# A state-space scan driven in place in its PSUM bank, in every iteration of a fused Mamba, attention and expert kernel

## The chip, the cores and the metric

The kernel runs on 1 core of one Trainium2 chip. The metric is the device time of one execution in microseconds (us). Before the change it is 1405.29 us, the median of 3 runs (1405.14 to 1409.21).

## The reference, cut to what matters

Eight images of 64 channels and 32x32 pixels go through three blocks: a selective state-space layer (Mamba) with group norm and residual, causal attention inside windows, and a mixture of eight experts of which each token takes two. The change lies in the first block, whose core is a recurrence over the 1024 tokens of an image, for 128 channels times 16 states:

```
def _selective_scan(xc, dt, Bmat, Cmat, A, D):
    def step(h, inp):
        dt_t, B_t, C_t, x_t = inp
        dA = jnp.exp(dt_t[..., None] * A)                        # "decay"
        dBx = dt_t[..., None] * B_t[:, None, :] * x_t[..., None] # "drive"
        h = dA * h + dBx                                         # "state"
        y = jnp.einsum('bdn,bn->bd', h, C_t)                     # "read", then "fold"
        return (h, y)
    ...
t = t + _L1_attn_ref(_ln_t(t), L1_attn_w_attn, L1_attn_w_proj)
t = t + _L1_ffn_ref(_ln_t(t), ...)
```

The 128 x 16 = 2048 recurrences of an image are 16 chunks of 128 rows, each row 1024 tokens long.

## The kernel before, in words

**A pipeline over images.** `pipeline` calls each engine's `program(a, c, p, b, f)` 12 times. In one iteration five images are in five stages: `c` is the image whose scan runs, `p` the one whose scan is being read out and normalised, `b` the one in attention, `f` the one in the experts. Eight images give iterations in which only some stages exist: in iterations 1 and 2 there is a scan without attention (`c` without `b`), in 3 scan and attention without experts, in 4 to 8 all of them, and from 9 on no scan.

**Two stages per iteration.** The first part of an iteration computes, step by step, row maxima of attention scores on VectorE (`row_maxima`, L979) with the front of the next scan beside them. The second part is the **scan stage**: a list of 28 rounds (`ROUNDS`), walked in the same order by TensorE, ScalarE and VectorE. Every engine runs its instructions strictly in the order written, and semaphores do the rest.

**What a round holds.** `UNITS_IN` gives the number of scan units per round (32 in all; a unit is half a chunk, 512 tokens). `TURNS` gives the expert image's pieces: output projection, layer norm, router, eight `expert` products, transposes. From round 4 on each round also has one of the 24 attention key steps (`KEY_STEPS`): four score matmuls, four exponentials, eight matmuls with the values.

**A unit.** TensorE spreads the rows of u over 128 partitions into a PSUM bank (L1353). VectorE multiplies them with B (the drive), then scans. ScalarE makes the decay of a chunk by an exponential (`decay_chunk`, L821), at the round of the chunk's first unit and behind three of that round's attention exponentials. GpSimd multiplies the finished state by C (`read`, L711); two state buffers alternate, so chunk k needs the read of chunk k-2.

There are two forms of it on VectorE. Without attention (`if b` false), `drive_in_bank` (L1037) writes the product over the bank itself, and `scan_half` (L1030) scans that bank at once; it waits for the `driven` count that the instruction in front of it raises, and for the chunk's decay. The second half starts from the last element of the first. With attention, `drive_unit` (L1054) writes the product to an SBUF buffer of three chunks, and `scan` (L1045) takes a whole chunk of 1024 tokens from there, one chunk late:

```
if h == 0 and k > 0:
    scan(k - 1)
```

so that it stands behind the first drive of the chunk after, and the last one behind all rounds (`scan(NJ - 1)`).

**The ring.** Five PSUM banks (`RING`) are handed out in the order in which TensorE uses them: to score tiles, units and turns alike. TensorE may write a bank when its user five places earlier has been read: a score by its exponential, an expert product by its multiplication on VectorE, a unit by `driven` (with attention) or `scanned` (without). Where the next user's bank isn't free, TensorE waits, and all of its later work with it.

## Time and profile before

| | |
|---|---|
| median of 3 runs | 1405.29 us |
| the profiled execution | 1405.26 us |
| its span, first to last instruction | 1403.4 us |
| mean granted TensorE clock | 0.856 |
| VectorE busy | 1116.6 us (80%) |
| TensorE matmul busy | 1032.5 us (74%) |
| ScalarE busy | 684.2 us (49%) |
| GpSimd busy | 487.1 us (35%) |

The span is the time from the first to the last instruction of one profiled execution; 1.86 us of that execution lie outside of it. Busy shares are averages over unlike stages, so the stage in question is read by itself: the timeline lists an engine's instructions in order with start, duration and, in brackets, the idle time before and what ended it; windows give the busy time of each engine in a stretch.

### The profile page before, as it was taken

The page shows a single profiled execution, that of the slowest core. Times are in us where ns is not written, and L with a number is a line of the kernel's source. Part 1 is how long each engine was busy: PE and PEld are TensorE (multiplying, and loading weights), DVE is VectorE, ACT ScalarE, POOL GpSimd, SP SyncE. Part 2 cuts the span into 40 slices and gives each one's busy share as a digit, 9 for nine tenths or more (in the row PEclk, how much of TensorE's full clock was granted, in tenths as well). Part 3 has the DMA queues.
Part 4 walks back from the last instruction along what each step waited for, and adds up shares of the span by engine and source line. Part 5 has one row for each costly group of instructions (what it writes and reads, how often), then busy time and mean ns, then how long its engine had stood idle before and what let it go on. Part 6 is the DMA issues. An engine that isn't in the chain of part 4 may idle for free.

```text
span 1403.4 us, 16864 instructions
## 1 busy us (share of the span) xinstructions
PE 1032.5 (74%) x6132; PEld 431.9 (31%) x6132; DVE 1116.6 (80%) x1398; ACT 684.2 (49%) x1178; POOL 487.1 (35%) x257
## 2 busy tenths in 40 slices
PE   3255325858886898779877998689868976986984
PEld 1001101323333333323333334233333333433442
DVE  5695359898899998999899989998999987258235
ACT  3324212438644774367446654576437702740660
POOL 3262336335442543353255334444425421000000
PEclk9557556979987999889987998899879997999895
DMA  2640583154425333534335433543154321120000
GB/s 45 165 120 31 124 169 82 40 143 123 100 64 141 97 80 90 134 91 110 72 96 125 117 82 81 123 115 81 51 135 104 81 58 41 35 50 1 2 16 8
DMA packets 40937, 120.25 MB, mean 86 GB/s; under 512 B 9222, under 2 KB 9610, under 8 KB 38475
## 3 DMA queue, kind: packets, MB, share of 16 engines
q1 hardware_dynamic: 27030, 68.83, 21.1%
q10 hardware_dynamic: 13824, 50.34, 14.4%
q8 instruction: 49, 0.80, 0.3%
q14 instruction: 34, 0.28, 0.1%
HBM read 95.65 MB, written 17.20 MB: 80 GB/s over the span
## 4 chain that ended last, share of the span: by engine, by line
DVE 39%; PE 28%; issue 9%; ACT 3%; POOL 2%; DMA 1%; DVEq 0%; ACTq 0%; SPq 0%
DVE row_max L979 16%; DVE state L1045 8%; PE ps L1436 6%; PE ps L1421 5%; DVE drive L1054 4%; PE ps L1304 3%; PE ps L1216 2%; PE ps L1196 2%; PE ps L1405 2%; ACT probs L866 2%; PE ps L1201 2%; DVE moe L1136 2%; PE ps L1207 1%; PE ps L1353 1%; PE ps L1424 1%
## 5 line engine op out<-in xcount | busy, mean ns | idle before, releaser
L711 POOL TENSOR_TENSOR read<-state,c_rep 128x1024 f32<-128x1024 f32 x128 | 311.3, 2434 | 365.5 <-DVE state L1045 271.9
L866 ACT ACTIVATE probs<-ps 128x512 f32<-128x512 f32 (+3 forms) x768 | 327.2, 499 | 109.2 <-PE ps L1424 79.1
L979 DVE TENSOR_REDUCE row_max<-ps 128x1 f32<-128x640 f32 (+7 forms) x352 | 328.8, 985 | 39.0 <-PE ps L1308 38.0
L1045 DVE TENSOR_TENSOR_SCAN state<-decay,drive 128x1024 f32<-128x1024 f32 x96 | 265.3, 2764 | 1.6 <-DVE drive L1054 1.2
L1421 PE MATMUL ps<-q_stack,k_stack 128*128 128x512 bf16 (+3 forms) x768 | 214.6, 345 | 65.4 <-DVE drive L1054 28.7
L1304 PE MATMUL ps<-k_stack,q_stack 128*128 128x512 bf16 (+3 forms) x704 | 200.0, 365 | 72.0 <-DVE row_max L979 70.0
L821 ACT ACTIVATE decay<-decay,a_scale 128x1024 f32<-128x1024 f32 x128 | 147.1, 1154 | 100.8 <-DMA decay<-dt_dram 100.8
L1353 PE MATMUL ps<-u_rows,pick 128*128 128x512 bf16 x256 | 113.1, 466 | 100.3 <-DVE state L1030 73.7
L1436 PE MATMUL ps<-probs,v_aug 128*32 128x512 f32 (+3 forms) x1536 | 168.2, 510 | 8.8 <-ACT probs L866 3.7
L1421 PEld LDWEIGHTS ps<-q_stack,k_stack 128*128 128x128 bf16 x768 | 75.9, 100 | 253.7 <-ACT probs L866 65.1
L1054 DVE TENSOR_TENSOR drive<-ps,b_rep 128x512 f32<-128x512 f32 x192 | 127.7, 678 | 21.0 <-PE ps L1353 19.3
L1304 PEld LDWEIGHTS ps<-k_stack,q_stack 128*128 128x128 bf16 x704 | 57.3, 103 | 200.5 <-DVE row_max L979 144.4
L1424 PE MATMUL ps<-mask_k,ident_bf 128*128 128x128 bf16 x512 | 106.9, 230 | 0.0
L1308 PE MATMUL ps<-mask_q,ident_bf 128*128 128x128 bf16 x448 | 103.6, 236 | 0.0
L661 POOL TENSOR_TENSOR ln_s<-ln_s,minus_half 128x8 f32<-128x8 f32 x16 | 26.3, 1645 | 219.8 <-DVE ln_s L961 219.2
L1216 PE MATMUL ps<-read,fold 128*32 128x512 f32 x512 | 75.2, 679 | 7.8 <-POOL read L711 7.8
L1353 PEld LDWEIGHTS ps<-u_rows,pick 128*128 128x128 bf16 x256 | 26.0, 105 | 170.2 <-DVE state L1030 104.9
L1405 PE MATMUL ps<-w_expert,xn_t 96*128 96x512 f32 x128 | 66.5, 629 | 0.0
L1136 DVE TENSOR_TENSOR moe<-ps,gate_e 128x512 f32<-128x512 f32 x64 | 43.6, 681 | 26.9 <-PE ps L1405 26.9
L1030 DVE TENSOR_TENSOR_SCAN state<-decay,ps 128x512 f32<-128x512 f32 x32 | 39.1, 1220 | 26.6 <-ACT decay L821 23.8
L1308 PEld LDWEIGHTS ps<-mask_q,ident_bf 128*128 128x128 bf16 x448 | 47.4, 106 | 36.0 <-issue 8.6
L1037 DVE TENSOR_TENSOR ps<-ps,b_rep 128x512 f32<-128x512 f32 x64 | 43.2, 674 | 16.5 <-PE ps L1353 16.5
(184 smaller groups left out, 1262.7 us busy)
## 6 DMA issues: line engine op xcount, KB each, us to landing
decay<-dt_dram ACTq DMA_DIRECT2D x96, 512.0 KB, 4.7
decay<-dt_dram SPq DMA_DIRECT2D x32, 512.0 KB, 6.1
q_stack<-q_parts_dram SPq DMA_DIRECT2D x48, 192.0 KB
k_stack<-k_parts_dram SPq DMA_DIRECT2D x48, 192.0 KB
u_rows<-read SPq DMA_DIRECT2D x96, 64.0 KB, 2.0
k_parts_dram<-read SPq DMA_DIRECT2D x40, 128.0 KB, 2.4
dt_dram<-read SPq DMA_DIRECT2D x8, 512.0 KB, 2.6
q_parts_dram<-read SPq DMA_DIRECT2D x24, 128.0 KB, 2.3
```

The costliest lines, as they stand in the source:

```text
L711: pool.tensor_tensor(read[:, k % (2 * NG), :], state[:, k % 2, :], c_rep[:, :], ALU.mult)\
L821: act.activation(decay[:, k % DECAYS, :], decay[:, k % DECAYS, :], ACT.Exp, scale=a_scale[:, j:j + 1]).then_inc(decayed.sem, 1)
L866: act.activation(probs[:, e % (2 * QUAD), 0:w], bank_of(("scores", e))[:, 0:w], ACT.Exp, scale=SCALE).then_inc(exped.sem, 1)
L979: dve.tensor_reduce(row_max[:, i, h0:h0 + nh], scores[:, :, 0:P * (i + 1)], AX.X, ALU.max, negate=True).then_inc(row_maxed.sem, 1)
L1045: dve.tensor_tensor_scan(state[:, k % 2, :], decay[:, k % DECAYS, :], drive[:, k % 3, :], 0.0, ALU.mult, ALU.add).then_inc(scanned.sem, NH)
L1054: dve.tensor_tensor(drive[:, k % 3, halves(h)], bank_of(("u", k2)), b_rep[:, halves(h)], ALU.mult)\
L1304: last = pe.matmul(ps[:, bank, 0:w], q_stack[:, h0 + hh, tokens(i)], k_stack[:, h0 + hh, h * BANK:h * BANK + w], start=True, stop=not diag ...
L1308: last = pe.matmul(ps[:, bank, w - P:w], ident_bf[:, :], mask_q[:, :], start=False, stop=True)
L1353: return pe.matmul(bank, pick[:, q, :, :].rearrange("p n e -> p (n e)"), rows[:, g, halves(k2 % 2)], start=True, stop=True)
L1421: last = pe.matmul(bank[:, 0:w], k_stack[:, head, tokens(j)], q_stack[:, head, lo:lo + w], start=True, stop=not diagonal)
L1424: last = pe.matmul(bank[:, 0:P], ident_bf[:, :], mask_k[:, :], start=False, stop=True)
L1436: last = pe.matmul(ps[GW * hq:GW * (hq + 1), ACC, lo:BANK], v_aug[:, j, quad * QUAD + hq, :], probs[:, (QUAD * s + hq) % (2 * QUAD), 0:BAN ...
```

## The change

In iterations 3 to 8 the scan now takes the form that iterations 1 and 2 have: `drive_in_bank(k2)` and `scan_half(k2)` for every unit. `drive_unit`, `scan` and the last `scan(NJ - 1)` are gone, and a unit's bank is free when it is `scanned`. The lists that order the rounds have new entries. ScalarE takes the attention values ahead of `take_t1` instead of behind `high_qk`, VectorE starts the first layer norm at step 27 instead of 26, and TensorE makes the group-mean product at step 12 instead of 13.

```diff
-        UNITS_IN = (4, 0, 2, 1, 2, 0, 2, 0, 2, 1, 2, 2, 0, 1, 2, 0, 1, 0, 1, 1, 2, 1, 2, 1, 1, 1, 0, 0)
-        FOLDS = ((0, 0, 13), (0, 1, 8), (1, 0, 20), (1, 1, 20))
-        TURNS = ((0, "attn_t", 0), (1, "attn_t", 1), (2, "proj", 0), (10, "xn_t", 0), (10, "xn_t", 1),
-                 (11, "router", 0), (13, "expert", 0), (16, "expert", 1), (16, "expert", 2), (18, "expert", 3),
+        UNITS_IN = (4, 0, 2, 1, 1, 0, 2, 1, 3, 1, 2, 1, 0, 1, 2, 0, 1, 0, 1, 1, 2, 1, 3, 1, 0, 1, 0, 0)
+        FOLDS = ((0, 0, 13), (0, 1, 8), (1, 0, 21), (1, 1, 20))
+        TURNS = ((0, "attn_t", 0), (1, "attn_t", 1), (3, "proj", 0), (9, "xn_t", 0), (9, "xn_t", 1),
+                 (10, "router", 0), (14, "expert", 0), (16, "expert", 1), (16, "expert", 2), (18, "expert", 3),
                  (19, "expert", 4), (20, "expert", 5), (23, "expert", 6), (23, "expert", 7), (26, "out_t", 0),
-                 (26, "out_t", 1))
+                 (27, "out_t", 1))
...
-        VARIANCE_AT, SCALE_AT, GATES_AT = 3, 7, 12
+        VARIANCE_AT, SCALE_AT, GATES_AT = 3, 7, 11
...
-            return {"early": (row_maxed, p), "u": (driven, c) if b else (scanned, c), ...
+            return {"early": (row_maxed, p), "u": (scanned, c), ...
...
-                                        (p, take_t1), (p, take_xn_t), (p, high_qk), (b, take_values), (p, mid_qk)):
+                                        (b, take_values), (p, take_t1), (p, take_xn_t), (p, high_qk), (p, mid_qk)):
...
-                        (22, p, gate_group_norm), (26, p, centre_first), (28, p, lambda: variance(0, p)))
+                        (22, p, gate_group_norm), (27, p, centre_first), (28, p, lambda: variance(0, p)))
...
                             for k2 in units:
-                                if b:
-                                    drive_unit(k2)
-                                else:
-                                    drive_in_bank(k2)
-                                    scan_half(k2)
+                                drive_in_bank(k2)
+                                scan_half(k2)
...
-                    if c and b:
-                        scan(NJ - 1)
...
-                        ((9, 11), p, out_projection), ((11, 12), c, dt_before_bias), ((13,), p, group_mean_product),
+                        ((9, 11), p, out_projection), ((11, 12), c, dt_before_bias), ((12,), p, group_mean_product),
```

Of the kernel before, what the change touches and what calls it, by code (L numbers as in the profile page):

```python
# [8 lines left out]
ALU = mybir.AluOpType  # L9
# [36 lines left out]
def mamba_attention_moe(nc, x, W_in, conv_w, conv_b, W_x, W_dt, b_dt, A_log, D, W_out, gn_gamma, gn_beta,  # L46
# [12 lines left out]
    NH = T // BANK  # L59
    QB = BANK // P  # L60
    CH = P // NS
    NJ = DI // CH
# [6 lines left out]
    DECAYS = 4  # L69
# [13 lines left out]
    with ExitStack() as ctx:  # L83
# [237 lines left out]
        def signal(name, per, base=0):  # L321
# [20 lines left out]

        UNITS_IN = (4, 0, 2, 1, 2, 0, 2, 0, 2, 1, 2, 2, 0, 1, 2, 0, 1, 0, 1, 1, 2, 1, 2, 1, 1, 1, 0, 0)
        FOLDS = ((0, 0, 13), (0, 1, 8), (1, 0, 20), (1, 1, 20))
        TURNS = ((0, "attn_t", 0), (1, "attn_t", 1), (2, "proj", 0), (10, "xn_t", 0), (10, "xn_t", 1),
                 (11, "router", 0), (13, "expert", 0), (16, "expert", 1), (16, "expert", 2), (18, "expert", 3),
                 (19, "expert", 4), (20, "expert", 5), (23, "expert", 6), (23, "expert", 7), (26, "out_t", 0),
                 (26, "out_t", 1))
        FIRST_SPREADS, SPREAD_LAG = 2, 2
        VARIANCE_AT, SCALE_AT, GATES_AT = 3, 7, 12  # L350
        BEFORE = len(UNITS_IN) - NKEY
# [114 lines left out]
        def halves(n):  # L466
            return slice(n * BANK, (n + 1) * BANK)
# [46 lines left out]
        def bank_read(user, c, p, b, f):  # L514

            kind, n = user
            return {"early": (row_maxed, p), "u": (driven, c) if b else (scanned, c), "scores": (exped, b), "heads": (attn_ready, b),
                    "attn_t": (attn_t_copied, f), "proj": (t2_ready, f), "xn_t": (xnt_copied[1], f),
                    "router": (gate_centred, f), "expert": (weighted, f), "out_t": (x_out_copied, f)}[kind] + (n + 1,)
# [30 lines left out]
        with nc.Block() as block:  # L550
# [170 lines left out]
            def _(act):  # L721
                def program(_, c, p, b, f):
# [82 lines left out]
                    for batch, work in ((c, silu_argument), (c, gate_tanh), (c, softplus_start), (c, take_b),  # L805
                                        (c, softplus_end), (p, group_norm), (c, take_c), (c, high_u), (c, mid_u),
                                        (p, take_t1), (p, take_xn_t), (p, high_qk), (b, take_values), (p, mid_qk)):
                        if batch:
                            work()
# [80 lines left out]
            def _(dve):  # L890
                def program(_, c, p, b, f):
# [83 lines left out]
                    def row_maxima(s):  # L975
# [11 lines left out]
                        (18, c and not b, lambda: less_high(dve, c)), (18, c and not b, lambda: less_mid(dve, c)),  # L987
                        (22, p, gate_group_norm), (26, p, centre_first), (28, p, lambda: variance(0, p)))
                    for s in range(NSCORE):
# [21 lines left out]
                    def bank_of(user):  # L1011
                        return banks(RING[places[user] % len(RING)])
# [21 lines left out]
                    def drive_in_bank(k2):  # L1034
# [3 lines left out]
                                          ALU.mult).then_inc(driven.sem, 1)  # L1038

                    def scan(k):  # L1040
                        dve.wait_ge(decayed.sem, decayed.at(c, k + 1))
                        dve.wait_ge(driven.sem, driven.at(c, 2 * k + 2))
                        if k >= 2:
                            dve.wait_ge(read_out.sem, read_out.at(c, k - 1))
                        dve.tensor_tensor_scan(state[:, k % 2, :], decay[:, k % DECAYS, :], drive[:, k % 3, :], 0.0,  # L1045
                                               ALU.mult, ALU.add).then_inc(scanned.sem, NH)

                    def drive_unit(k2):

                        k, h = k2 // 2, k2 % 2  # L1050
                        dve.wait_ge(u_rep.sem, u_rep.at(c, k2 + 1))
                        if k >= 3:
                            dve.wait_ge(scanned.sem, scanned.at(c, NH * (k - 2)))
                        dve.tensor_tensor(drive[:, k % 3, halves(h)], bank_of(("u", k2)), b_rep[:, halves(h)],  # L1054
                                          ALU.mult)\
                           .then_inc(driven.sem, 1)
                        if h == 0 and k > 0:
                            scan(k - 1)

# [95 lines left out]
                    for n, (s, units, turns) in enumerate(ROUNDS):  # L1155
                        if c:
                            for k2 in units:
                                if b:
                                    drive_unit(k2)
                                else:  # L1160
                                    drive_in_bank(k2)
                                    scan_half(k2)
                        if f:
# [5 lines left out]
                        if b and s is not None and s - LAG in LAST_STEP:  # L1169
                            divide_heads(LAST_STEP.index(s - LAG))  # L1170
                    if c and b:
                        scan(NJ - 1)
                    if p:
# [9 lines left out]
            def _(pe):  # L1183
# [8 lines left out]
                def program(_, c, p, b, f):  # L1192
# [100 lines left out]
                    def score_step(s):  # L1293
# [20 lines left out]
                        ((1, 1), c, convolution), ((0, 2, 4, 5), p, last_folds), ((6, 8), c, gate_projection),  # L1314
                        ((9, 11), p, out_projection), ((11, 12), c, dt_before_bias), ((13,), p, group_mean_product),
                        ((14, 15), c, b_product), ((17, 20), c, c_product), ((24,), b, value_projection),
# [196 lines left out]
```

## Rows read from the trace of the kernel before

**Rows 1.** The page: chain that ended last, shares of the span by engine.
```profile
DVE 39%; PE 28%; issue 9%; ACT 3%; POOL 2%; DMA 1%; DVEq 0%; ACTq 0%; SPq 0%
```

**Rows 2.** Windows of the scan stages of iterations 3 and 5: us, busy (instructions), clock.
```profile
301.74:377.51 75.77, 58.00 (x451) 21.94 (x451) 68.18 (x56) 56.53 (x115) 35.52 (x15) 0.93 0.50 120
587.93:676.72 88.79, 75.61 (x523) 31.64 (x523) 82.80 (x96) 60.60 (x122) 38.89 (x16) 0.91 0.42 102
```

**Rows 3.** The same two windows, instructions of line L1045 alone, VectorE busy.
```profile
301.74:377.51 75.77, 47.72 (x16) 0.93 0.50 120
587.93:676.72 88.79, 43.53 (x16) 0.91 0.42 102
```

**Rows 4.** Timeline of VectorE, iteration 5: start, us, engine, line, form.
```profile
590.88 2.28 DVE L1045 TENSOR_TENSOR_SCAN state<-decay,drive 128x1024 f32<-128x1024 f32 x1
593.08 1.26 DVE L1054 TENSOR_TENSOR drive<-ps,b_rep 128x512 f32<-128x512 f32 x2
...
604.50 1.29 DVE L1054 TENSOR_TENSOR drive<-ps,b_rep 128x512 f32<-128x512 f32 x2
605.70 2.28 DVE L1045 TENSOR_TENSOR_SCAN state<-decay,drive 128x1024 f32<-128x1024 f32 x1
```

**Rows 5.** Timeline of VectorE, iteration 1, where no attention runs.
```profile
100.58 0.67 DVE L1037 TENSOR_TENSOR ps<-ps,b_rep 128x512 f32<-128x512 f32 x1
101.34 1.22 DVE L1030 TENSOR_TENSOR_SCAN state<-decay,ps 128x512 f32<-128x512 f32 x1
102.48 0.67 DVE L1037 TENSOR_TENSOR ps<-ps,b_rep 128x512 f32<-128x512 f32 x1
...
104.44 0.67 DVE L1037 TENSOR_TENSOR ps<-ps,b_rep 128x512 f32<-128x512 f32 x1
```

**Rows 6.** Three lines: count, ns min/median/max, first and last start in us.
```profile
L1030 DVE TENSOR_TENSOR_SCAN state<-decay,ps x32: 1219/1221/1221, 50.7 to 239.6; 128x512 f32<-128x512 f32 x32
...
L1045 DVE TENSOR_TENSOR_SCAN state<-decay,drive x96: 2278/2390/4324, 304.1 to 1120.3; 128x1024 f32<-128x1024 f32 x96
...
L711 POOL TENSOR_TENSOR read<-state,c_rep x128: 2342/2360/3882, 54.0 to 1124.2; 128x1024 f32<-128x1024 f32 x128
```

**Rows 7.** VectorE groups, 587.93 to 667.87 us: busy us, mean ns, idle.
```profile
L1045 DVE TENSOR_TENSOR_SCAN state<-decay,drive 128x1024 f32<-128x1024 f32 x14 | 37.4, 2674 | 0.0
```

**Rows 8.** Waits of VectorE, 587.93 to 667.87 us: total us, times, longest.
```profile
DVE drive L1054 <- PE ps L1353: 3.2, 5, 1.1
DVE den L1068 <- PE ps L1446: 0.5, 1, 0.5
DVE moe L1136 <- PE ps L1405: 0.5, 1, 0.5
DVE gate_m L1095 <- ACT gate_e L841: 0.3, 1, 0.3
```

**Rows 9.** Timeline of VectorE: the last expert product of iteration 5.
```profile
667.19 0.68 DVE L1136 TENSOR_TENSOR moe<-ps,gate_e 128x512 f32<-128x512 f32 x1
```

**Rows 10.** Timeline of TensorE, end of the same stage.
```profile
668.48 0.33 PE L1421 MATMUL ps<-q_stack,k_stack 128*128 128x384 bf16 x1
...
669.98 0.39 PE L1353 MATMUL ps<-u_rows,pick 128*128 128x512 bf16 x1 [0.68 <-DVE drive L1054]
...
677.56 0.66 PE L1446 MATMUL ps<-ident,acc_sb 128*128 128x128 f32 x4 [0.70 <-ACT acc_sb L855]
```

**Rows 11.** Timelines of TensorE and VectorE in iteration 5: one unit.
```profile
609.45 0.38 PE L1353 MATMUL ps<-u_rows,pick 128*128 128x512 bf16 x1
...
609.87 0.69 DVE L1054 TENSOR_TENSOR drive<-ps,b_rep 128x512 f32<-128x512 f32 x1 [0.58 <-PE ps L1353]
```

**Rows 12.** Lines L821 and L759 as in rows 6; one wait, over the whole span.
```profile
L821 ACT ACTIVATE decay<-decay,a_scale x128: 1131/1149/1199, 49.5 to 1115.4; 128x1024 f32<-128x1024 f32 x128
...
L759 ACT ACTIVATE xn<-xcen x16: 624/629/630, 149.0 to 1370.0; 128x512 f32<-128x512 f32 x16
...
DVE ln_s L947 <- PE ps L1246: 8.0, 8, 3.7
```

More of the change, by code:

```diff
@@ L516, in bank_read @@
             kind, n = user
-            return {"early": (row_maxed, p), "u": (driven, c) if b else (scanned, c), "scores": (exped, b), "heads": (attn_ready, b),
+            return {"early": (row_maxed, p), "u": (scanned, c), "scores": (exped, b), "heads": (attn_ready, b),
                     "attn_t": (attn_t_copied, f), "proj": (t2_ready, f), "xn_t": (xnt_copied[1], f),
@@ L1038, in drive_in_bank @@
                                           ALU.mult).then_inc(driven.sem, 1)
[L1040 to L1058, printed above, removed]
                     def divide_heads(n):
```

## The prediction, made before the changed kernel was run

> **What bounds the kernel now.** I read the chain of waits first: VectorE holds 39% of it, TensorE 28%, nothing else comes near [rows 1]. Then the windows of the scan stage, the only part whose instructions change. In iteration 5 it lasts 88.79 us, of which VectorE is busy 82.80, TensorE 75.61, ScalarE 60.60 and GpSimd 38.89 [rows 2]; it stands for the five of iterations 4 to 8. So VectorE sets its length. Iteration 3, without experts, is looser: 68.18 of 75.77. Then the single instructions on VectorE, in the old form [rows 4] and in the form that now comes everywhere [rows 5], and last the end of the stage, where TensorE takes over [rows 9, 10].
>
> **VectorE, per chunk.** Old form: two drives take 1.20 us from the start of the first to the start of the scan (604.50 to 605.70), an undisturbed scan 2.20 to the start of the next (590.88 to 593.08) [rows 4]: 3.40. But scans run from 2.28 to 4.32 us [rows 6]: their two inputs both lie in SBUF, and they stretch where GpSimd is reading a state. In iteration 5 they take 43.53 us, 7.05 over 16 x 2.28 [rows 3]. A stage costs 16 x 3.40 + 7.05 = 61.45.
>
> New form, as iteration 1 shows it: drive to scan 0.76, scan to next drive 1.14, and for the second half 1.96 from drive to drive; two halves take 104.44 - 100.58 = 3.86 [rows 5]. Every first half-scan there takes 1.219 to 1.221 us although GpSimd's reads of 2.36 us run beside them [rows 6], so I add nothing for contention. A stage costs 16 x 3.86 = 61.8. What the scan wins (two halves of 1.22 and 1.28 against a mean of 2.72) is taken back by the wait of each scan for the product just in front: 0.76 against 0.60, 32 times, and by the split. The sum is 0.3 us, nothing. In iteration 3 the old scans take 47.72, so 16 x 3.40 + 11.24 = 65.6 against 61.8: VectorE wins 3.8 there.
>
> The Trainium skill, page "VectorE: DVE Perf Modes", section "The DRAIN you can't avoid", says that a chain of copies with a semaphore after each took as long as one without, so that the wait costs nothing extra. Here 0.76 stands against 0.60; the trace disagrees for this pair, perhaps because those copies don't depend on each other. By the page a half would cost 0.16 less, 5.1 us per stage; what that would make of the time is the third rival.
>
> **What can't be hidden any more: the end of the stage.** The old form had a store of VectorE work that nobody's bank waits for. The last expert product is multiplied at 667.19 to 667.87 [rows 9]. By then VectorE had done 30 drives and 14 scans, 37.4 us of them [rows 7]: 30 x 0.60 + 14 x 2.20 + (37.4 - 14 x 2.28 = 5.5) = 54.3. The last two drives and two scans, to 676.7, ran beside TensorE's last rounds. In the new lists unit 30 comes in round 23, ahead of experts 6 and 7, and only unit 31 behind them. So 31 halves precede the same point: 31 x 1.93 = 59.8, which is 5.5 more.
>
> TensorE's way from there to the end of attention is fixed by its own order: from unit 31 at 669.98 (it waited 0.68 for the drive that freed its bank) to the last transposes at 677.56 are 7.58 us of scores, exponentials and values [rows 10]. In the new ring the first score of round 25 takes the bank of expert 7, so this tail starts as soon as that is multiplied: 0.66 for the three scores ahead of unit 31 (668.48 to some 669.14 in the old order) plus 7.58 plus 0.05 for the hand-over is 8.3, against 677.56 - 667.87 = 9.7 before. That gives back 1.4. In the tail VectorE has one half (1.93) and the early maxima left and then idles; before, it was full to the end.
>
> **VectorE's idle time before that point.** Old: 3.2 + 0.5 + 0.5 + 0.3 = 4.5 us [rows 8]. Walking the rounds with the new lists, what changes:
> - At the start the longest wait for a unit (1.1) [rows 8] vanishes, for the half-scan of unit 0 now stands there: -1.1.
> - The output projection's turn moves from round 2 to 3, and the layer norm's variance follows in the same round; between them is ScalarE's square, 0.63 [rows 12], formerly beside unit 6 and its scan. With two hand-overs +0.9.
> - Chunk 4 starts in round 6 (unit 8 was in round 4), its decay on ScalarE stands behind three exponentials, and its scan now needs it at once instead of a chunk later. A decay is 1.15 [rows 12]; the drive (0.67) covers a part. GpSimd's read of chunk 2 comes about as late. +1.0. Later decays have work in front of them on VectorE and cost 0 to 1 each; I take 0.
> - Units that take the bank of the unit before: 4 in the old ring, 10 in the new (7, 11, 14, 17, 19, 26, 30 and those of the start). The bank comes free after the scan and not after the drive, and until the next unit is there 0.05 and 0.42 us pass (609.45 to 609.87) [rows 11]. Where other VectorE work stands between, it is covered; ahead of 14 and 19 little does. +1.0.
>
> Together 4.5 + 1.8 = 6.3. It can't be under 0; 14 is what all ten round trips (4.7) and a decay wait of about 1 in five rounds would make of 4.5.
>
> **Sum.** One stage of iterations 4 to 8: +5.5 - 1.4 + 1.8 = +5.9, from -0.4 (no idle) to +13.6 (14). Five stages: +29.5. Iteration 3: VectorE wins 3.8, but it idles 7.6 there already and the round trips grow; I take -2, from -4 to +3. Iterations 1 and 2 keep their form and the order of their units; a fold one round later has its reads long before: 0. In the row-maxima part VectorE waits 8.0 us in 8 times for the transposes ahead of the layer norm [rows 12]; one step later hides between none and all of it, but the variance is then one step nearer to its square. The attention values are copied ahead of a square that waits for step 27 anyway, and no step before that needs ScalarE in between; without that cover it would be one copy per iteration, at most the 1.15 of rows 12. The group mean one step earlier can hold TensorE for VectorE's statistics. These, and the turns that shift in iterations 9 to 11, I take as 0, from -8 to +8. All in all +27.5.
>
> The sum is made on the profiled execution, 1405.26 us, of which 1403.4 is the span. The median of the runs is 1405.29, so it stands for both: 1432.8, say 1433.
>
> **Rivals.**
> 1. The store was no help: TensorE hands over units so early that VectorE hardly idles, idle 0 to 1. For it: TensorE is busy 75.61 of 88.79 and waits more for VectorE than the other way. Against it: 4.5 us of idle in the old form, whose banks came free sooner. At 0.5 a stage costs 5.5 - 1.4 - 4.0 = +0.1; five stages 0.5, iteration 3 -2: 1404. That is within 0.3%, which is about what a measurement of this kernel can tell from no change.
> 2. The ring becomes the bound: round trips and decays are exposed everywhere, idle 14. Then +13.6 x 5 + 3 = +71, 1476. For it: ScalarE's decays lose a chunk's slack. Against: ten expert and layer-norm pieces fill the gaps.
> 3. The other side: the wait for the own product costs nothing where expert work stands between, and the sum of busy time counts. Price 0.76 - 0.60 = 0.16 a half [rows 4, 5], from the first stage with attention on: 31 x 0.16 = 5.0 off the 59.8, so a stage is +5.5 - 5.0 - 1.4 + 0 (idle as before) = -0.9; iteration 3 -3.8 - 5.1 = -8.9. Together -13.4, 1392. For it: the 7.05 us of stretched scans go for certain. Against it: in the new order nothing stands between a product and its scan in any round, as in rows 5.
>
> That the change doesn't do what it says is excluded: its form already runs in two iterations.
>
> **How the numbers follow.** Forecast, 1410 to 1453: 0.64. Rival 2, above 1453 and up to 1476: 0.10. Rival 1, 1401 to 1409: 0.13. Rival 3, below 1401: 0.13. So slower 0.74, same 0.13, faster 0.13. The forecast's own range is 1410 to 1453; for 8 in 10 it reaches to rival 1 and to some of 3: 1398 to 1453.
>
> **What would show it.** Right: half-scans of 1.22 and 1.28 us in all stages, two halves 3.86 apart where VectorE has work; GpSimd's reads all near 2.36; the scan stages of iterations 4 to 8 longer by about 6, with idle VectorE behind the last expert product; waits of VectorE for the unit's matmul and for the decay. Wrong: stages no longer than 89 us, or a drive followed by its scan after 0.60.

## The result and the profile after

The changed kernel takes 1457.65 us (median of 4 runs, 1455.97 to 1459.66) against 1406.8 us for the kernel before in the same comparison (4 runs, 1405.14 to 1409.21): a ratio of 1.0368, interval 1.0344 to 1.0391. That is slower by some 51 us, where 27.5 were forecast. It lies 5 us above the upper end of the range. The profiled execution took 1457.25 us with a span of 1455.5, 52.1 more than before.

First the page, engine by engine: busy us, share of the span, instructions. This is the kernel after.

```profile
PE 1038.8 (71%) x6039; PEld 434.4 (30%) x6132; DVE 1097.9 (75%) x1494; ACT 688.9 (47%) x1178; POOL 477.0 (33%) x257
```

VectorE is busy for 18.7 us less than before (1116.6). TensorE's matmuls are busy for 6.3 us more, although the trace of after holds 93 matmul records fewer (6039 for 6132). So for VectorE the 52 us are waiting, on an engine that has less to do.

The instructions themselves came out as forecast: count, then ns as min, median, max, over the whole span of the kernel after.

```profile
L1030 DVE TENSOR_TENSOR_SCAN state<-decay,ps x128: 1219/1220/1222, 52.5 to 1163.6; 128x512 f32<-128x512 f32 x128
L1030 DVE TENSOR_TENSOR_SCAN state<-decay,state,ps x128: 1278/1280/1281, 54.4 to 1169.0; 128x512 f32<-128x512 f32 x128
```

```profile
L711 POOL TENSOR_TENSOR read<-state,c_rep x128: 2341/2355/2387, 55.9 to 1170.4; 128x1024 f32<-128x1024 f32 x128
```

No scan stretches any more, and GpSimd's longest read is 2387 ns instead of 3882 [rows 6].

Next the windows from a stage's first drive to the row maxima behind it, in iterations 3 and 5: length, then busy us and instructions of TensorE, its weight loads, VectorE, ScalarE and GpSimd, then granted clock, DMA share, GB/s. The kernel before (these windows run on to the row maxima, those of [rows 2] only to the last scan's end):

```profile
301.74:383.26 81.52, 63.14 (x483) 23.72 (x487) 70.41 (x60) 58.63 (x117) 37.88 (x16) 0.94 0.52 122
587.93:682.70 94.77, 80.88 (x555) 33.43 (x559) 85.02 (x101) 62.73 (x125) 41.25 (x17) 0.92 0.46 107
```

The kernel after:

```profile
303.78:394.09 90.31, 65.89 (x476) 23.68 (x487) 64.21 (x77) 59.12 (x117) 37.74 (x16) 0.91 0.48 111
608.00:710.01 102.01, 82.47 (x547) 34.51 (x559) 82.28 (x116) 63.58 (x125) 39.30 (x17) 0.92 0.42 99
```

Length less VectorE's busy time is its idle time. In iteration 3 VectorE works 6.2 us less (70.41 to 64.21) and idles 15.0 us more (11.1 to 26.1). In iteration 5 it works 2.7 less and idles 10.0 more (9.7 to 19.7). The granted clock is 0.94 and 0.91 in iteration 3 and 0.92 both times in iteration 5. TensorE's matmuls in iteration 3 take 2.75 us more, for the same work.

From these windows the 52.1 us of the span add up so: iteration 3 +8.8; iterations 4 to 8 +6.6, +7.2, +6.9, +8.5 and +6.9, together +36.1; the row maxima behind iteration 3 +3.15 (54.79 to 57.94); the start +2.0; the end +1.65; elsewhere 0.4. The start isn't the change's: the first drive begins at 46.59 us before and at 48.61 after, but in the ten kernels below it begins either at 46.3 to 46.6 (eight of them) or at 48.1 to 48.2 (two), the latter also where nothing but one step of GpSimd is moved.

**Who waits for whom in iteration 3.** TensorE's waits in the stage: us in total, times, longest. The kernel before:

```profile
PE ps L1421 <- DMA q_stack<-max_parts_dram: 9.6, 1, 9.6
PE ps L1421 <- DVE drive L1054: 3.6, 3, 1.8
...
PE ps L1353 <- DVE drive L1054: 1.4, 2, 1.1
```

The kernel after:

```profile
PE ps L1396 <- DMA q_stack<-max_parts_dram: 8.0, 1, 8.0
PE ps L1328 <- DVE state L1030: 7.1, 7, 1.4
PE ps L1396 <- DVE state L1030: 7.0, 11, 1.5
```

TensorE waited 5.0 us for drives in 5 waits; now it waits 14.1 us for half-scans in 18. (The wait for a DMA at the top is there before and after.) VectorE's waits for units there went from 4.4 us to 8.5. New are 3.3 for decays, 2.6 for one more unit and 2.7 ahead of the early maxima. Each engine waits for the other in turn. This is how it looks in the timeline of both engines (start, duration, instruction, idle time before it), the kernel after:

```profile
324.19 0.38 PE L1328 MATMUL ps<-u_rows,pick 128*128 128x512 bf16 x1
...
325.01 1.22 DVE L1030 TENSOR_TENSOR_SCAN state<-decay,ps 128x512 f32<-128x512 f32 x1 [0.97 <-ACT decay L821]
326.14 0.68 DVE L1037 TENSOR_TENSOR ps<-ps,b_rep 128x512 f32<-128x512 f32 x1
326.29 0.23 PE L1396 MATMUL ps<-q_stack,k_stack 128*128 128x128 bf16 x1 [1.49 <-DVE state L1030]
```

The unit of 324.19 is in its bank early; but the next score needs the bank that the half-scan of 325.01 reads. That scan waits 0.97 for its decay, and TensorE stands still for 1.49 until it ends. Before, the drive in SBUF would have freed that bank before the decay was there.

### The profile page after: what moved, and what is told of

Read it like the earlier page. It is cut to its first block and busy times, and to the rows that moved or that the text cites. A ratio compares the mean times of both kernels' runs of the same rounds, so it can differ in the third digit from the quotient of the medians.

```text
span 1455.5 us, 16728 instructions
## 1 busy us (share of the span) xinstructions
PE 1038.8 (71%) x6039; PEld 434.4 (30%) x6132; DVE 1097.9 (75%) x1494; ACT 688.9 (47%) x1178; POOL 477.0 (33%) x257
## 3 DMA queue, kind: packets, MB, share of 16 engines
HBM read 95.65 MB, written 17.20 MB: 78 GB/s over the span
## 5 line engine op out<-in xcount | busy, mean ns | idle before, releaser
L711 POOL TENSOR_TENSOR read<-state,c_rep 128x1024 f32<-128x1024 f32 x128 | 301.5, 2357 | 383.3 <-DVE state L1030 304.3
L1396 PE MATMUL ps<-q_stack,k_stack 128*128 128x512 bf16 (+3 forms) x724 | 207.5, 345 | 56.8 <-DVE state L1030 37.6
L1279 PE MATMUL ps<-k_stack,q_stack 128*128 128x512 bf16 (+3 forms) x672 | 187.3, 357 | 66.0 <-DVE row_max L979 62.5
L1037 DVE TENSOR_TENSOR ps<-ps,b_rep 128x512 f32<-128x512 f32 x256 | 174.5, 682 | 54.3 <-PE ps L1328 39.9
L1328 PE MATMUL ps<-u_rows,pick 128*128 128x512 bf16 x239 | 106.1, 470 | 138.1 <-DVE state L1030 121.5
L821 ACT ACTIVATE decay<-decay,a_scale 128x1024 f32<-128x1024 f32 x128 | 147.0, 1154 | 108.8 <-DMA decay<-dt_dram 106.7
L1030 DVE TENSOR_TENSOR_SCAN state<-decay,ps 128x512 f32<-128x512 f32 x128 | 156.2, 1220 | 46.1 <-ACT decay L821 36.0
L1030 DVE TENSOR_TENSOR_SCAN state<-decay,state,ps 128x512 f32<-128x512 f32 x128 | 163.8, 1280 | 12.3 <-ACT decay L821 0.4
L1283 PE MATMUL ps<-mask_q,ident_bf 128*128 128x128 bf16 x448 | 100.2, 229 | 17.7 <-DVE row_max L979 17.7
L1283 PEld LDWEIGHTS ps<-mask_q,ident_bf 128*128 128x128 bf16 x448 | 46.3, 103 | 37.1 <-issue 10.5
L1399 PEld LDWEIGHTS ps<-mask_k,ident_bf 128*128 128x128 bf16 x512 | 53.1, 104 | 12.4 <-issue 10.4
```

The lines of the kernel that those rows point to most:

```text
L711: pool.tensor_tensor(read[:, k % (2 * NG), :], state[:, k % 2, :], c_rep[:, :], ALU.mult)\
L821: act.activation(decay[:, k % DECAYS, :], decay[:, k % DECAYS, :], ACT.Exp, scale=a_scale[:, j:j + 1]).then_inc(decayed.sem, 1)
L1030: dve.tensor_tensor_scan(state[:, k % 2, halves(h)], decay[:, k % DECAYS, halves(h)], bank_of(("u", k2)), state[:, k % 2, BANK - 1:BANK] i ...
L1037: dve.tensor_tensor(bank_of(("u", k2)), bank_of(("u", k2)), b_rep[:, halves(k2 % 2)], ALU.mult).then_inc(driven.sem, 1)
L1279: last = pe.matmul(ps[:, bank, 0:w], q_stack[:, h0 + hh, tokens(i)], k_stack[:, h0 + hh, h * BANK:h * BANK + w], start=True, stop=not diag ...
L1283: last = pe.matmul(ps[:, bank, w - P:w], ident_bf[:, :], mask_q[:, :], start=False, stop=True)
```

## The experiments

Two theories to begin with. The first: the new form itself costs the time, because it gives up two kinds of slack: the scan that came one chunk late, and the bank that was free after the drive instead of after the scan. The second: the new lists cost it, whatever the form. All ratios are against runs of the kernel before on the same chip, whose median was 1404.3 to 1405.6.

**1. The lists without the form, and the form without the lists.** The first takes every changed list and order of the diff and leaves `drive_unit`, late `scan` and the release by `driven`; the second does the reverse:

```diff
-            return {"early": (row_maxed, p), "u": (driven, c) if b else (scanned, c), ...
+            return {"early": (row_maxed, p), "u": (scanned, c), ...
...
-                                if b:
-                                    drive_unit(k2)
-                                else:
-                                    drive_in_bank(k2)
-                                    scan_half(k2)
+                                drive_in_bank(k2)
+                                scan_half(k2)
...
-                    if c and b:
-                        scan(NJ - 1)
```

> The kernel before with the new lists and the three moved steps, but the old form (SBUF drive, whole-chunk scan one chunk late). Theory A (the new form costs: a scan that must follow its drive at once leaves VectorE without work in store, so it idles for the next unit and the next decay, iteration 3 included): the old form stands the new lists, 1400 to 1420 us, scan stages of iterations 4 to 8 of 93 to 97 us up to the next row maxima, against 94.8 before. Theory B (the lists cost): 1440 us or more.

> The changed kernel with the old lists and the old places of the three steps: the form alone. Theory A: 1455 to 1480 us, at least what the whole change takes, since the new lists were spread so that units come earlier for the new form. Theory B (the lists cost): 1400 to 1420 us.

Measured: lists alone 1464.92 us, ratio 1.0425 (1.0383 to 1.0467); form alone 1465.55, ratio 1.0426 (1.0393 to 1.0459). Both together are 1457.65. So the form costs some 60 us by itself, as the first theory wants it. But the lists alone cost as much, which that theory had denied. VectorE's waits in iteration 5 of the lists alone:

```profile
DVE drive L1054 <- PE ps L1353: 7.9, 7, 4.1
```

7.9 us for units, with one wait of 4.1, against 3.2 and 1.1 [rows 8]. That wait is for unit 8, which the new lists put in round 6 instead of 4, and TensorE had stood still before it:

```profile
619.18 0.50 PE L1421 MATMUL ps<-q_stack,k_stack 128*128 128x384 bf16 x1 [2.08 <-ACT probs L866]
...
624.30 0.69 DVE L1054 TENSOR_TENSOR drive<-ps,b_rep 128x512 f32<-128x512 f32 x1 [4.14 <-PE ps L1353]
```

With the form given, the lists win 8 us back (1465.55 to 1457.65); but with the lists given, the form wins 7 back (1464.92 to 1457.65). So neither theory holds as it stands, and this pair of runs alone can't say which of the two the loss belongs to: either is enough by itself. The stages tell more. Iteration 3 grows by 2.6 us with the lists alone (81.52 to 84.16), by 7.0 with the form alone (88.51) and by 8.8 with both: there it is mostly the form. Iteration 5 grows by 10.7 (94.77 to 105.48), 10.4 (105.15) and 7.2.

**2. One kind of slack alone: the scan not late.** The kernel before, its scan of a chunk right behind the chunk's own second drive; banks free after the drive, as before.

```diff
-                        if h == 0 and k > 0:
-                            scan(k - 1)
+                        if h == 1:
+                            scan(k)
...
-                    if c and b:
-                        scan(NJ - 1)
```

> The kernel before with one thing changed: the whole-chunk scan stands right behind the second drive of its own chunk and not one chunk late. Drive in SBUF, banks free when driven, as before. Theory A (the lateness is the store that hides VectorE's waits): +6 us a stage (own wait 0.16 to 0.3 x 16, a decay or unit wait here and there, 2.3 us of scan moved ahead of the last expert product), about 1445 us. Theory C (what costs is the bank held until the scan is over): no more than 1412 us, for banks come free as before.

Measured: 1475.19 us, ratio 1.0498 (1.0466 to 1.0531). The lateness is worth 70 us, more than either expectation. Iteration 3 grows by 4.4 us, iteration 5 by 14.2. VectorE's waits in iteration 5:

```profile
DVE drive L1054 <- PE ps L1351: 7.7, 6, 2.3
...
DVE moe L1136 <- PE ps L1403: 3.7, 2, 2.5
DVE state L1045 <- DVE drive L1054: 2.4, 12, 0.2
```

The scan is the work that VectorE does while TensorE makes the next unit. With it in front, VectorE waits 7.7 us for units and 3.7 for experts. Its wait for its own product is small beside that: 0.2 a time.

**3. The other kind alone: the bank held.** The kernel before, with one wait more on TensorE: the bank of an even unit comes free only when the scan behind its drive has ended. VectorE's instructions and their order stay as they were.

```diff
                             pe.wait_ge(read_by.sem, read_by.at(batch, count))
+                            kind, k2 = users[place - len(RING)]
+                            if b and kind == "u" and k2 % 2 == 0 and k2 > 0:
+                                pe.wait_ge(scanned.sem, scanned.at(c, NH * (k2 // 2)))
```

> The kernel before, VectorE's order untouched, but TensorE may reuse the bank of an even unit only when the scan behind its drive (that of the chunk before) is over too: every second unit's bank is held about 2.2 us longer, 1.1 us on the mean, as much as the new form holds it. If the longer hold by itself starves the ring: iteration 3 longer by 4 us or more, stages 4 to 8 by 3 or more, 1425 to 1445 us. If it is the missing store of late scans that costs, and TensorE's longer waits are hidden while VectorE has a scan in hand: 1405 to 1413 us.

Measured: 1469.03 us, ratio 1.0454 (1.0416 to 1.0492), above both expectations. The windows of iterations 3 and 5:

```profile
299.69:389.73 90.04, 62.74 (x476) 23.66 (x487) 66.03 (x60) 58.81 (x117) 37.86 (x16) 0.92 0.48 111
604.83:710.47 105.64, 82.37 (x547) 35.29 (x559) 82.76 (x101) 62.61 (x125) 41.26 (x17) 0.89 0.41 95
```

Iteration 3 is as long as in the changed kernel (90.04 against 90.31), VectorE idle 24.0 of it, with the old form, the old lists and the late scan all in place. TensorE's waits in the stage of iteration 5:

```profile
PE ps L1424 <- DVE state L1045: 12.4, 8, 2.9
PE ps L1353 <- DVE state L1045: 3.9, 2, 2.5
```

And VectorE's:

```profile
DVE drive L1054 <- PE ps L1353: 11.0, 11, 2.2
```

TensorE waits at least 16.3 us for scans, and as a consequence VectorE 11.0 for units. So this half of the first theory holds too: to hold a bank for one scan longer is enough, alone, for a loss as large as the whole change's.

**4. What the form gives back.** The changed kernel, but with the product written to SBUF halves, the half-scan reading them, and the bank free after the drive.

```diff
-            return {"early": (row_maxed, p), "u": (scanned, c), ...
+            return {"early": (row_maxed, p), "u": (driven, c) if b else (scanned, c), ...
...
-                                               bank_of(("u", k2)), state[:, k % 2, BANK - 1:BANK] if h else 0.0,
+                                               drive[:, k % 3, halves(h)] if b else bank_of(("u", k2)),
+                                               state[:, k % 2, BANK - 1:BANK] if h else 0.0,
...
-                        dve.tensor_tensor(bank_of(("u", k2)), bank_of(("u", k2)), b_rep[:, halves(k2 % 2)],
+                        product = drive[:, k2 // 2 % 3, halves(k2 % 2)] if b else bank_of(("u", k2))
+                        dve.tensor_tensor(product, bank_of(("u", k2)), b_rep[:, halves(k2 % 2)],
```

> The changed kernel, new lists, half-scans right behind their products as in it, but in iterations 3 to 8 the product goes to the old SBUF buffer and the bank is free when driven. If the bank held until the scan is over is what costs (TensorE waits 14.8 us a stage for scans): iteration 3 falls from 90.3 to about 85 us up to the next row maxima, stages 4 to 8 from 102 to 97 or below even with some stretched scans (both inputs in SBUF again, at most 7 us); 1425 to 1445 us. If it is the scan's place right behind its drive that costs (no store of work, as in the run with the scan not late, where banks came free when driven and the time was 70 us over before): no better than 1450 us, and 1455 to 1475 with the stretched scans.

Measured: 1544.63 us, ratio 1.0989 (1.0965 to 1.1013). No expectation held that, and it was no test of the bank. The half-scans with both inputs in SBUF, count and ns:

```profile
L1030 DVE TENSOR_TENSOR_SCAN state<-decay,drive x96: 1223/2830/2915, 302.0 to 1254.2; 128x512 f32<-128x512 f32 x96
L1030 DVE TENSOR_TENSOR_SCAN state<-decay,state,drive x96: 1282/1284/2496, 303.9 to 1261.1; 128x512 f32<-128x512 f32 x96
```

One of them in the timeline, with GpSimd's read:

```profile
332.69 2.37 POOL L711 TENSOR_TENSOR read<-state,c_rep 128x1024 f32<-128x1024 f32 x1 [3.12 <-DVE state L1030]
...
333.28 2.86 DVE L1030 TENSOR_TENSOR_SCAN state<-decay,drive 128x512 f32<-128x512 f32 x1
```

GpSimd begins to read the finished chunk just before the next chunk's first half-scan starts. 67 of the 96 first halves are stretched (1.46 us or more), 29 aren't (1.22 to 1.23). The read ends at 335.06, the scan at 336.14; that is 1.08 later, close to the 1.22 of an undisturbed one, as if it had run only then. The means are 2172 and 1406 ns, so the 192 halves cost 96 x (2172 - 1220) + 96 x (1406 - 1280) = 103 us more than in the changed kernel, and the whole is 87 us longer. This is about what reading the product from PSUM saves in this order: with its second input in PSUM the half-scan isn't held. It may be a part of why the change costs less than its two losses alone.

**5. Mending the changed kernel.** Three edits, each against one of its waits. First, ScalarE makes each decay one unit earlier:

```diff
-                                if k2 % 2 == 0:
-                                    decay_chunk(k2 // 2)
+                                if k2 == 0:
+                                    decay_chunk(0)
+                                if k2 % 2 == 1 and k2 < UNITS - 1:
+                                    decay_chunk(k2 // 2 + 1)
```

> The changed kernel with each chunk's decay made at the round of the unit before the chunk instead of at its first unit. Theory A with decays as the larger part of the idle time: VectorE's waits for decays (about 3 us a stage in the changed kernel) go, 1436 to 1446 us. If the waits for decays only stand in front of waits for units, so that the next unit is late then: 1453 to 1461 us.

Measured: 1452.49 us, ratio 1.0349 (1.0302 to 1.0395), between the two expectations. VectorE's waits for decays in the scan stages are gone, but little is won: iterations 3, 4, 6 and 7 are 0.9 to 1.4 us shorter, iterations 5 and 8 are 1.4 and 0.8 longer. There waits for units grew instead, in iteration 5 from 4.8 us to 7.6. Of the 6.6 us by which the span is shorter, 2.1 are the start (46.54 for 48.61), which isn't the edit's, and 2.8 the row maxima behind iteration 3 (57.94 to 55.11). Second, the last unit but one two rounds later, so that it no longer precedes experts 6 and 7, and the last unit one round later:

```diff
-        UNITS_IN = (4, 0, 2, 1, 1, 0, 2, 1, 3, 1, 2, 1, 0, 1, 2, 0, 1, 0, 1, 1, 2, 1, 3, 1, 0, 1, 0, 0)
+        UNITS_IN = (4, 0, 2, 1, 1, 0, 2, 1, 3, 1, 2, 1, 0, 1, 2, 0, 1, 0, 1, 1, 2, 1, 3, 0, 0, 1, 1, 0)
```

> The changed kernel with unit 30 in round 25 and unit 31 in round 26, so that both stand behind the last expert product and beside TensorE's last rounds. If VectorE's work ahead of that product sets the end of the stage, 1.9 us of it go in each of the five stages with experts, nothing comes back: 1444 to 1450 us. If TensorE's last rounds grow by the unit that they now wait for (unit 31 stands beside the last values): 1453 to 1462 us.

Measured: 1476.92 us, ratio 1.0507 (1.0483 to 1.0531): a miss, 19 us above the changed kernel. Its stages of iterations 4 to 8 take 103 to 108 us. In iteration 5 the part behind the last expert product grows by 4.3 us (13.76 to 18.03): there VectorE waits 3.7 us for the two late units and a decay, and TensorE 1.9 for their scans. Third, the old form in iteration 3 alone, where no experts run (release, drive and scan of the kernel before under `b and not f`):

```diff
                             for k2 in units:
-                                drive_in_bank(k2)
-                                scan_half(k2)
+                                if b and not f:
+                                    drive_unit(k2)
+                                else:
+                                    drive_in_bank(k2)
+                                    scan_half(k2)
```

> The changed kernel with the old form in iteration 3 alone (attention without experts), new lists everywhere. If iteration 3 loses to the form what its stage shows (90.3 us against 84.2 with the old form and the same lists), and the row maxima behind it fall back to 54.9 from 57.9: 1447 to 1453 us. If the later stages shift to make it up: 1455 us or more.

Measured: 1449.09 us, ratio 1.0307 (1.0261 to 1.0352), as expected. Iteration 3 takes 85.1 us instead of 90.3: of its +8.8, 5.2 go with the form. Holding banks, on the old lists, was worth 8.5 there (81.52 to 90.04, experiment 3). One part of the expectation missed: the row maxima behind iteration 3 didn't get shorter (57.94 us).

**6. Is there anything to win from the kernel before?** Two small edits of it. The in-bank form for the first two chunks alone, where banks are plentiful; and GpSimd's inverse root one chunk later, out of the way of reads.

```diff
-                                if b:
+                                if b and k2 >= 4:
                                     drive_unit(k2)
```

```diff
-                        if f and k == 1:
+                        if f and k == 2:
                             inverse_root(1, f)
```

> The kernel before, with the in-bank form for the first two chunks of an attention iteration alone (units 0 to 3, in round 0, before any score asks for a bank), and the old form behind them. If the form only costs where scores and units share the ring: VectorE's wait of 1.1 us at the start of the stage is covered and the stretched second scan (3.57) goes, 0.5 to 1.5 us in six stages: 1397 to 1402 us. If the store of a late scan counts there too: 1406 to 1415 us.

> The kernel before, with GpSimd's inverse root of the layer norm behind the read of chunk 2 and not of chunk 1. In the trace of before read 2 waits for it and runs into the scans of chunks 3 and 4 (3.88 us, the scan 4.14). If that stretch sits on VectorE's path: 1 to 2 us in each of five stages, 1396 to 1402 us. If the scaled layer norm then comes late (its scaling stands in round 7): 1405 us or more.

Measured: 1406.56 us, ratio 1.0013 (0.9997 to 1.0029), and 1405.13, ratio 0.9997 (0.9981 to 1.0014). Neither differs from before. No version that was run beats it.

## Why the prediction was wrong

**What held.** The change was slower, and for reasons that the prediction named. Half-scans of 1.22 and 1.28 us; a chunk in 3.88 us (609.94 to 613.82) for 3.86 forecast; reads near 2.36. In a stage of iterations 4 to 8 each term has the forecast sign. For iteration 5, from the first drive at 608.00 to the end of the last expert product, and on to the transposes:

```profile
609.94 0.68 DVE L1037 TENSOR_TENSOR ps<-ps,b_rep 128x512 f32<-128x512 f32 x1
610.70 1.28 DVE L1030 TENSOR_TENSOR_SCAN state<-decay,state,ps 128x512 f32<-128x512 f32 x1
611.90 0.67 DVE L1037 TENSOR_TENSOR ps<-ps,b_rep 128x512 f32<-128x512 f32 x1
612.68 1.22 DVE L1030 TENSOR_TENSOR_SCAN state<-decay,ps 128x512 f32<-128x512 f32 x1
613.82 0.67 DVE L1037 TENSOR_TENSOR ps<-ps,b_rep 128x512 f32<-128x512 f32 x1
...
624.55 0.69 DVE L958 TENSOR_REDUCE ln_s<-xn 128x8 f32<-128x512 f32 x1 [0.69 <-ACT xn L759]
...
629.97 0.70 DVE L1037 TENSOR_TENSOR ps<-ps,b_rep 128x512 f32<-128x512 f32 x1 [2.56 <-PE ps L1328]
631.47 1.22 DVE L1030 TENSOR_TENSOR_SCAN state<-decay,ps 128x512 f32<-128x512 f32 x1 [0.80 <-ACT decay L821]
...
695.57 0.68 DVE L1116 TENSOR_TENSOR moe<-ps,gate_e 128x512 f32<-128x512 f32 x1
...
703.18 1.89 DVE L1018 TENSOR_REDUCE row_max<-ps 128x4 f32<-128x512 f32 x3 [3.39 <-PE ps L1314]
```

```profile
704.87 0.66 PE L1421 MATMUL ps<-ident,acc_sb 128*128 128x128 f32 x4 [0.71 <-ACT acc_sb L855]
```

| term, iteration 5 | forecast | measured |
|---|---|---|
| VectorE's work up to the last expert product | +5.5 | +4.8 (75.4 to 80.25) |
| its idle time up to there | +1.8 | +3.5 (4.5 to 8.0) |
| from there to the transposes | -1.4 | -1.07 (9.69 to 8.62: 696.25 to 704.87) |
| sum | +5.9 | +7.2 |

The square's wait (0.69, forecast 0.9 with hand-overs) and the decay of chunk 4 (0.80, forecast 1.0) stand where they were put; VectorE idles at the end (3.39 ahead of the early maxima), as forecast. Too small was the idle time. VectorE's waits up to the last expert product:

```profile
DVE ps L1037 <- PE ps L1328: 4.8, 5, 2.6
DVE state L1030 <- ACT decay L821: 2.2, 4, 0.8
```

The decays came to 2.2, for the one of 1.0 that was counted. The waits for units are 4.8 against 3.2 before [rows 8], where the items "-1.1" and "+1.0" had left 3.1. More than half of them is the wait for unit 8 (2.56), and that one isn't for a held bank:

```profile
623.89 0.63 ACT L759 ACTIVATE xn<-xcen 128x512 f32<-128x512 f32 x1 [7.65 <-DVE xcen L952]
...
625.06 0.50 PE L1396 MATMUL ps<-q_stack,k_stack 128*128 128x384 bf16 x1 [2.08 <-ACT probs L866]
...
629.55 0.38 PE L1328 MATMUL ps<-u_rows,pick 128*128 128x512 bf16 x1
```

ScalarE waits 7.65 for the centred values before it makes the layer norm's square, and the exponentials of the first scores stand behind the square. So TensorE waits 2.08 for a score that has to leave its bank, and unit 8 comes only 4.5 us after that wait. The lists alone, with banks free after the drive, show the same 2.08 ahead of the same unit (experiment 1). The item of the square (+0.9) had priced what it costs VectorE, and nothing of what it costs TensorE and by that the next unit. The other four waits for units make 2.2 us, against 2.1 before without the one at the start: of the item of the ring ("+1.0") hardly anything shows here. Five stages came to +36.1 for 29.5: 6.6 of the miss.

**The step that failed** is iteration 3: "VectorE wins 3.8 there", "the round trips grow; I take -2, from -4 to +3". VectorE's work did fall, by 6.2. But the stage grew by 8.8, since VectorE's idle time grew by 15.0. That is 10.8 of the 24.6 us between 27.5 and 52.1, and it lies outside the bounds that I gave. It is the mechanism of the second rival, the ring as the bound, in one stage. What I held against that rival was "ten expert and layer-norm pieces fill the gaps", and iteration 3 has none of these. Its [rows 2] even show the looser stage; I read the room on VectorE as room for waits, when waits and work come in turn there and not side by side. I had counted only what passes when a bank has come free (0.05 and 0.42 us, [rows 11]), and not that it comes free a scan later, nor that the scan in between may wait for its decay. And I had counted only units that take a unit's bank: of TensorE's 14.1 us of waits for half-scans in iteration 3, 7.0 stand ahead of scores. Experiment 3 shows the price: bank-holding alone makes iteration 3 as long as it became. Experiment 5 shows that 5.2 of the 8.8 go with the form; the lists in the old form alone made 2.6 (experiment 1).

**The third term**, the 0 for the rest, holds the remaining 7.2: 2.0 at the start, which isn't the change's, 1.65 at the end and 3.15 in the row maxima behind iteration 3, within the bounds of -8 to +8. The row maxima stay open. The kernel after, windows there:

```profile
423.00:433.00 10.00, 6.26 (x32) 3.29 (x32) 8.46 (x11) 2.63 (x4) 6.27 (x5) 0.50 0.30 74
433.00:443.00 10.00, 8.80 (x42) 4.71 (x42) 8.59 (x10) 1.01 (x1) 0.76 (x1) 0.74 0.48 125
```

The kernel before:

```profile
412.00:422.00 10.00, 8.01 (x39) 4.13 (x40) 8.70 (x12) 2.05 (x3) 7.08 (x5) 0.53 0.29 71
422.00:438.05 16.05, 10.56 (x53) 4.46 (x51) 15.40 (x19) 6.56 (x7) 4.25 (x2) 0.93 0.50 122
```

TensorE is at or near its lower level (0.50 and 0.53 of full speed, 1.2 GHz) in one stretch of both kernels, and stays below full speed for longer after (0.74 over the next 10 us, where before it was 0.93 over the next 16). VectorE there waits for score matmuls. It isn't tied to the form in iteration 3 (57.94 with the old form there), and the lists alone don't bring it (55.09 with them in the old form). Row maxima of 57.1 to 57.3 us stand behind other iterations too, in the kernels of experiments 4 and 5 (behind iteration 4 in the one, behind 7, 2 and 5 in the others). What starts it wasn't found.

**The third rival** (the own product's wait free where other work stands between) was wrong: in the stage of iteration 5, with expert work, a scan still follows its product after 0.76 to 0.80 us (609.94 to 610.70, 611.90 to 612.68).

**Shown and only argued.** Shown: each kind of slack, taken alone, is enough for the loss (70 and 64 us against some 51), and so are the form alone and the lists alone (60 each); in iteration 3 the form makes the larger part, and holding the banks alone makes as much. Argued: that the losses don't add up because the same overlap of TensorE and VectorE can be lost only once, and because the unstretched scans (7.05 us in iteration 5, 11.24 in iteration 3, by the prediction's count) come off the sum. No run separates these two, and none says how the loss of iterations 4 to 8 divides between form and lists.

Open is also what TensorE's clock adds in the experiments. Over iteration 5 the granted clock is 0.92 in both kernels, but 0.87 with the lists alone and with the form alone, 0.88 in experiment 2 and 0.89 in experiment 3. What goes with that shows inside one kernel, the first edit of experiment 5, iterations 5 and 6:

```profile
599.83:703.20 103.37, 84.69 (x547) 35.43 (x559) 82.44 (x116) 63.01 (x125) 39.28 (x17) 0.87 0.42 98
758.08:858.52 100.44, 80.74 (x547) 34.07 (x559) 82.31 (x116) 62.75 (x125) 39.28 (x17) 0.92 0.42 102
```

The first edit of experiment 6 shows 95.65 us at 0.88 (iteration 4) and 94.88 at 0.92 (iteration 5). By these pairs, as an estimate, 1 to 3 of the 10 to 14 us that the stages of experiments 1 to 3 grow by may be the clock's. That leaves most of each loss standing, but not the order of 51, 60 and 64, nor the 7 and 8 us of experiment 1. Iteration 3 of experiment 3 is free of it: its clock is 0.92, and its matmuls take 62.74 us for 63.14 before.

## What to carry to other kernels

In a ring of buffers, price a consumer by how long it holds its buffer, not only by how long it works: one scan of 2.2 us more per pair of units cost 64 us here, with VectorE's own instructions and their order untouched. A consumer that runs one piece late is a store of work for the times when its producer isn't ready; keep it unless something else fills them, and look at the stage that has nothing else by itself. Try a new form and its lists of order apart and together before one of them is blamed, and ask of an instruction that moves which other engine's work stands behind it: here a square on ScalarE held up exponentials, these a score, and the score a unit.

## What the runs showed of the hardware

A half-scan with both inputs in SBUF that meets GpSimd's read takes up to 2.92 us (the median of 96 is 2.83) instead of 1.22, while one with its product in PSUM takes 1.219 to 1.222 in all 128 cases. The Trainium skill, page "SBUF — State Buffer", section "SBUF: two separate sides", says that a VectorE instruction with two SBUF inputs and a GpSimd instruction that reads SBUF exclude each other for their whole length; as an estimate by it, the scan of 333.28 (experiment 4) would end 1.22 after the read's end, at 336.28. Measured: 336.14, and the trace agrees. That a change of order can cost so much by this was the surprise: 67 of 96 first halves are stretched, 50 of them by 1.6 us or more, and all halves together lose 103 us. In the old order 48 of 96 scans took more than 2.4 us, and all together lost 46 (265.3 less 96 x 2.28).
